# Seven sub-convolutions at the points of a polynomial product, in place of nine even/odd ones

## The reference

```
xc = x.T
h  = relu(bn1(conv1d(xc, conv1_w, kernel 1)))
h  = bn2(conv1d(h, conv2_w, kernel 17, pad 8))
x_conv = relu(h + xc).T
A  = exp(-dist(x @ w_se.T + b_se)) * adj ;  x_nmp = A @ relu(x @ w_msg.T + b_msg)
y  = GRU gates of [x_conv, x_nmp] against x          # tanh and sigmoid, three gates
x  = layernorm(x + y)
x  = layernorm(x + relu(((1 + eps) x + adj @ x) @ W1 + b1) @ W2 + b2)
```

## Time and profile before

| | us |
|---|---|
| median of 3 runs (393.55 to 393.71) | 393.56 |
| the profiled execution | 394.27 |
| its span, first to last instruction | 392.5 |
| TensorE / VectorE / ScalarE / GpSimd busy | 377.3 / 280.3 / 232.9 / 230.3 |
| one full step | 46.3 |
| start of step 1, end of step 7 | 36.9, 359.7 |

### The profile page before, as it was taken

How to read it: one execution, slowest core, us unless ns; L and a number is a source line. 1 busy time by engine, 2 the same in 40 slices (tenths; PEclk the granted TensorE clock), 3 DMA queues, 4 the chain that set the end, 5 groups by cost and what they waited for, 6 DMA issues and landing times.

```text
span 392.5 us, 6585 instructions
## 1 busy us (share of the span) xinstructions
PE 377.3 (96%) x2329; PEld 336.0 (86%) x2329; DVE 280.3 (71%) x545; ACT 232.9 (59%) x422; POOL 230.3 (59%) x217
## 2 busy tenths in 40 slices
PE   2999999999999999999999999999999999999974
PEld 2988989898889989899898988899898998988954
DVE  4999958864787658867598657885588675857564
ACT  3663584557654675737655478446766476462773
POOL 4886446574484934946366655657349483475343
PEclk9999999999999999999999999999999999999999
DMA  7503001201102101301012010120112110000011
GB/s 239 210 2 108 3 0 56 107 2 53 53 12 100 41 15 53 109 0 54 0 53 107 0 53 5 48 107 12 44 53 61 48 56 0 3 0 2 0 55 53
DMA packets 7991, 19.39 MB, mean 49 GB/s; under 512 B 672, under 2 KB 5024, under 8 KB 6944
## 3 DMA queue, kind: packets, MB, share of 16 engines
q1 hardware_dynamic: 7536, 18.50, 13.3%
q10 hardware_dynamic: 432, 0.59, 0.5%
HBM read 14.89 MB, written 4.19 MB: 49 GB/s over the span
## 4 chain that ended last, share of the span: by engine, by line
PE 95%; DVE 2%; DMA 1%; ACT 1%; POOL 0%; issue 0%; SPq 0%; ACTq 0%; DVEq 0%
PE conv L1129 31%; PE back L1129 30%; PE front L1231 7%; PE back L1231 7%; PE back L1320 6%; PE conv L1183 5%; PE front L1203 3%; PE front L1223 2%; PE back L1282 2%; DMA xv<-in_x_dram 1%; PE conv L1203 1%; PE front L1213 1%; PE front L1320 1%; ACT tail L693 1%; DVE xn L945 1%; PE front L1129 0%
## 5 line engine op out<-in xcount | busy, mean ns | idle before, releaser
L1129 PE MATMUL conv<-sth,wh 128*128 128x256 f32 x280 | 85.4, 305 | 0.0
L1129 PE MATMUL conv<-stl,wh 128*128 128x256 f32 x280 | 79.9, 285 | 0.0
L1129 PE MATMUL conv<-sth,wl 128*128 128x256 f32 x280 | 79.8, 285 | 0.0
L501 POOL TENSOR_TENSOR rstd<-rstd,minus_half 128x4 f32<-128x4 f32 (+1 forms) x34 | 36.1, 1063 | 60.6 <-DVE rstd L927 60.6
L506 POOL TENSOR_TENSOR xw<-xw,xv 128x512 f32<-128x512 f32 (+1 forms) x17 | 20.9, 1230 | 59.0 <-ACT xw L677 59.0
L1129 PEld LDWEIGHTS conv<-sth,wh 128*128 128x128 f32 x280 | 52.9, 189 | 1.6
L1129 PEld LDWEIGHTS conv<-stl,wh 128*128 128x128 f32 x280 | 52.9, 189 | 0.6
L1129 PEld LDWEIGHTS conv<-sth,wl 128*128 128x128 f32 x280 | 52.9, 189 | 0.0
L519 POOL TENSOR_TENSOR amat<-amat,adjT 128x512 f32<-128x512 f32 x32 | 48.8, 1547 | 0.8
L1231 PE MATMUL front<-amat,msg 128*128 128x256 f32 x128 | 30.2, 379 | 0.0
L1231 PE MATMUL back<-adjT,xn 128*128 128x256 f32 x120 | 29.2, 385 | 0.8 <-DVE xn L945 0.8
(11 more groups left out here) (217 smaller groups left out, 1018.5 us busy)
## 6 DMA issues: line engine op xcount, KB each, us to landing
adjT<-in_adj_dram SPq DMA_DIRECT2D x8, 1024.0 KB, 4.8
out_dram<-tail SPq DMA_DIRECT2D x15, 256.0 KB, 2.2
xv<-in_x_dram SPq DMA_DIRECT2D x7, 512.0 KB, 3.3
gbuf<-in_gates_dram SPq DMA_DIRECT2D x1, 576.0 KB, 7.0
tail<-in_conv_dram ACTq DMA_DIRECT2D x2, 256.0 KB, 3.7
xv<-in_x_dram SPq DMA_DIRECT2D x2, 256.0 KB, 4.7
later_w<-in_later_dram SPq DMA_DIRECT2D x1, 452.0 KB, 6.3
tail<-in_conv_dram SPq DMA_DIRECT2D x1, 320.0 KB, 5.3
```

The source lines that it names most:

```text
L501: done(pool.tensor_tensor(rstd[:, k, h, q], rstd[:, k, h, q], minus_half[:, q], ALU.pow), RSTD[k])
L1129: ins = pe.matmul(bank, a, b, start=first and k == 0, stop=last and k == len(todo) - 1)
```

## The change

The nine sub-convolutions become seven, by evaluating four-coefficient polynomials (four token phases, and the 17 taps in four phases) at 0, 1, -1, 2, -2, 1/2 and infinity. `NTAP` becomes (5, 5, 5, 5, 5, 5, 4): 34 taps. The streams are linear combinations of the phases of h1: `token_diffs` (two subtractions of 544 elements) and the sums and differences of `streams1`/`streams2` on GpSimd; `half_stream`, `zero_stream`, `parts2`, `parts1`, `inf_stream` on VectorE; five pairs of `stream_high` (ScalarE) and `stream_low` (VectorE) split them. The results are recombined with scales (`sc`, bn2's scale times constants) in `u_sum`, `pair2_sum`, `pair2_add`, `pair1_sum`, `pair1_add` and `inf_add` on VectorE, from two banks that ScalarE copies out twice each with different scales (`minus2_out`, `minus1_out`). The taps of each point are combined in the prologue (`taps_step`, and four sums on GpSimd). `hh` and `hl` move into the memory of `nmph` and `nmpl`. The lists of all engines are rewritten around it. Reference, DMAs of a step, gates, norms and MLP stay.

```diff
-NTAP = (5, 5, 4, 5, 5, 4, 4, 4, 4)
+HALF, ZERO, PLUS2, MINUS2, PLUS1, MINUS1, INF = range(7)
+POINTS = (0.5, 0.0, 2.0, -2.0, 1.0, -1.0)
+NTAP = (5, 5, 5, 5, 5, 5, 4)
...
+CONV_AT = ((0, 0), (0, 1), (1, 0), (1, 1), (2, 0), (2, 1), (1, 0))
...
 # GpSimd
+            def token_diffs(g, k0=0):
+                wait(pool, H1_READY, g, 2)
+                wait(pool, RI_READY, g - 1, 1)
+                (av[0:2] = h1[.., 1] - h1[.., 0];  av[2:4] = one_on(h1[.., 0]) - h1[.., 1])
+            def pair_streams(g, k, a, b, ready):
+                wait(pool, LS_READY, g - 1, (4, 3)[k - 1])
+                wait(pool, CONV_FULL[(MINUS1, MINUS2)[k - 1]], g - 1, 1)
+                (sv[r] = b + a;  sv[r + 1] = b - a)
 def steady:
+                streams1(gm)
                 residual(gb, 1 - u, 0)
-                split_diff(gm, 2)
                 residual(gb, 1 - u, 1)
...
                     mask(gm, u, b)
+                if front:
+                    token_diffs(s + 1)
                 rsqrt(1, gb, 0)
+                if front:
+                    streams2(s + 1)
                 rsqrt(1, gb, 1)
-                    (split_diff 0, diff_a, split_diff 1, diff_b)
...
 # ScalarE
+            def minus2_out(g):
+                wait(act, CONV_FULL[MINUS2], g, 1)
+                wait(act, ADD2_READY, g - 1, 2)
+                for k in range(2):
+                    done(act.activation(pm2[:, :, k, :], conv_out(MINUS2), ACT.Copy,
+                                        scale=sc[:, SC_MINUS2 + k:SC_MINUS2 + k + 1]), PM2_READY)
 def steady:
-                mm_out(gm)
                 for k in range(3):
                     msg_out(gm, k)
-                odd_high(gm, 1)
                 gates(gb, 0)
-                diff_high(gm, 1)
+                stream_high(gm, 3)
                 factors_out(gm)
                 gates(gb, 1)
-                odd_high(gm, 2)
-                diff_high(gm, 2)
-                am_out(gm)
+                minus2_out(gm)
+                stream_high(gm, 4)
                 if front:
                     x_high(gf, 1 - u)
-                bm_out(gm)
+                minus1_out(gm)
                 exps(gm, 0)
                 exps(gm, 1)
-                xconv_high(gm, 0)
                 h_high(gb, 0)
                 h_high(gb, 1)
+                xconv_high(gm, 0)
                 exps(gm, 2)
                 exps(gm, 3)
                 hidden(gb, 0)
                 hidden(gb, 1)
                 if front:
                     h1_out(gf, 0)
+                    h1_out(gf, 1)
+                    stream_high(gf, 0)
+                    stream_high(gf, 1)
                 nmp_high(gm, 0)
...
 # VectorE
+            def u_sum(g, u):
+                wait(dve, CONV_FULL[HALF], g, 1)
+                wait(dve, CONV_FULL[ZERO], g, 1)
+                (four scalar_tensor_tensor: usum phase k = HALF * scale k + x phase k; one adds ZERO to phase 0)
+            def pair2_sum(g):
+                wait(dve, PM2_READY, g, 2)
+                (two scalar_tensor_tensor: pm2[k] += PLUS2 * scale k)
 def steady:
+                parts1(gm)
+                u_sum(gm, u)
                 for k in range(3):
                     messages(gm, k)
                 factors(gm)
-                odd_low(gm, 1)
                 gates(gb, 1 - u, 0)
-                diff_low(gm, 1)
+                stream_low(gm, 3)
                 gates_end(gb, 0)
-                m_sum(gm)
+                inf_stream(gm)
                 gates(gb, 1 - u, 1)
                 y_stats(gb, 0)
-                odd_low(gm, 2)
+                pair2_sum(gm)
                 gates_end(gb, 1)
                 y_apply(gb, 0)
+                pair2_add(gm)
                 y_stats(gb, 1)
-                diff_low(gm, 2)
-                x_sum(gm, u, 0)
+                stream_low(gm, 4)
                 y_apply(gb, 1)
-                x_sum(gm, u, 1)
-                g_sum(gm, 0)
-                pre_sum(gm, 0)
+                pair1_sum(gm)
                 h_low(gb, 0)
                 h_low(gb, 1)
-                xconv_low(gm, 0)
+                pair1_add(gm, 0)
                 (x_low(gf) 0 and 1)
+                pair1_add(gm, 1)
+                xconv_low(gm, 0)
                 out_stats(gb, 0)
                 out_stats(gb, 1)
+                (if front: half_stream, zero_stream, stream_low 0, parts2, stream_low 1, all of gf)
                 nmp_low(gm, 0)
+                inf_add(gm)
+                (if front: stream_low(gf, 2))
+                nmp_low(gm, 1)
+                xconv_low(gm, 1)
...
 # TensorE
 def steady:
-                (taps 0, 1, 2)
+                (taps HALF, ZERO, PLUS2)
                 (messages, gates(gb, 0), factors, gates(gb, 1), y_transpose(gb, 0))
-                taps(gm, 3)
-                taps(gm, 4)
+                taps(gm, MINUS2)
+                taps(gm, PLUS1)
                 y_transpose(gb, 1)
-                taps(gm, 5)
-                taps(gm, 6)
+                taps(gm, MINUS1)
                 (distances 0 and 1, aggregate(gb, 0))
-                taps(gm, 7, 0, 2)
+                taps(gm, INF, 0, 1)
                 (aggregate(gb, 1), distances 2 and 3)
-                taps(gm, 7, 2, 3)
+                taps(gm, INF, 1, 2)
                 mlp1(gb, 0)
                 mlp1(gb, 1)
+                (conv1(gf, 0), mlp2(gb, 0), conv1(gf, 1), mlp2(gb, 1), nmp(gm, 0))
+                taps(gm, INF, 2)
+                nmp(gm, 1)
```

More of the change, by code:

```diff
@@ new lines, in pair2_sum, with pair2_add @@
+            def pair2_sum(g):
+                wait(dve, PM2_READY, g, 2)
+                for k in range(2):
+                    done(dve.scalar_tensor_tensor(pm2[:, :, k, :], conv_out(PLUS2), sc[:, SC_PLUS2 + k:SC_PLUS2 + k + 1],
+                                                  pm2[:, :, k, :], ALU.mult, ALU.add), SD2_READY)
+            def pair2_add(g):
+                wait(dve, SD2_READY, g, 2)
+                wait(dve, U_READY, g, 5)
+                u01, u23 = (graph_rows(usum[:, :, :, :])[:, q, :, :] for q in range(2))
+                both = pm2[:, :, :, :].rearrange("p b r m -> p (b r) m")
+                done(dve.tensor_tensor(u01, u01, both, ALU.add), ADD2_READY)
+                done(dve.scalar_tensor_tensor(u23, both, 4.0, u23, ALU.mult, ALU.add), ADD2_READY)
@@ L897, in xconv_low, with inf_add @@
+            def inf_add(g):
+                wait(dve, CONV_FULL[INF], g, 1)
+                wait(dve, PRE_READY, g, 2)
+                done(dve.scalar_tensor_tensor(phase(usum[:, :, :, :], 3), conv_out(INF), sc[:, SC_INF:SC_INF + 1],
+                                              phase(usum[:, :, :, :], 3), ALU.mult, ALU.add), PRE_READY)
             def xconv_low(g, par):
@@ L1018, in prologue @@
                     messages(0, k)
+                taps_step(utaps[:, 0:4, :], w2, 4.0, w0)
+                taps_step(ataps[:, 5:9, :], w3, 4.0, w1)
+                taps_step(gtaps[:, 5:9, :], ataps[:, 5:9, :], 2.0, utaps[:, 0:4, :])
+                taps_step(ataps[:, 5:9, :], ataps[:, 5:9, :], -2.0, utaps[:, 0:4, :])
+                parts1(0)
                 factors(0)
-                tap_low(0)
+                tap_low(ZERO)
+                tap_low(HALF)
+                dve.wait_ge(tap_sums, steps[0])
+                u_sum(0, 0)
                 x_low(1, 1, 0)
                 x_low(1, 1, 1)
-                tap_low(1)
-                tap_low(2)
-                m_sum(0)
+                tap_low(PLUS2)
+                inf_stream(0)
+                pair2_sum(0)
+                pair2_add(0)
+                tap_low(PLUS1)
                 w_low_part(wl[:, S_GATE:S_GATE + 9, :], graw, wh[:, S_GATE:S_GATE + 9, :], w_count("gates"))
                 w_low_part(w1l[:, :], w1raw, w1h[:, :], w_count("w1"))
-                x_sum(0, 0, 0)
-                x_sum(0, 0, 1)
-                g_sum(0, 0)
-                pre_sum(0, 0)
-                tap_low(3)
-                tap_low(6)
-                odd_low(1, 0)
+                pair1_sum(0)
+                pair1_add(0, 0)
+                pair1_add(0, 1)
+                half_stream(1)
+                zero_stream(1)
                 xconv_low(0, 0)
-                diff_low(1, 0)
+                stream_low(1, 0)
+                parts2(1)
+                stream_low(1, 1)
                 nmp_low(0, 0)
+                inf_add(0)
                 dve.wait_ge(consts_loaded, 16)
```

558 lines of the change are left out of this document (279 added, 279 removed).

## The result

| | before | after |
|---|---|---|
| median, us | 393.63 (393.55 to 394.52, 4 runs) | 428.98 (428.78 to 429.13, 4 runs) |
| span of the profiled execution | 392.5 | 427.0 |
| start of step 1 | 36.9 | 46.7 |
| a full step | 46.30 | 49.54 |

The changed kernel takes 1.0892 times as long (95% interval 1.0873 to 1.0911): 35.4 us more, with the forecast at 420.0 and its own band at 412 to 426. TensorE does less and the kernel is slower. The page after, to be laid beside the earlier trace rows: first the busy times, then the last chain by engine.

A forecast was written before the change was run, and what follows sets the result against it. TensorE was taken to bound the kernel, 96% busy. Forecast: 393.56 + 15.4 (seven steps) + 8.1 (first group) + 2.4 (step 1) + 0.5 (end) = 420.0 us; forecast band 412 to 426, range 405 to 430.

The forecast's parts named there:

- saved on TensorE, a step: Matmuls of each step: 40 taps become 34, saving 2.2 us a step, 15.5 in seven steps.
- wait 1: Second y_transpose: TensorE waits 1.4 us a step because pair2_sum stands ahead of gates_end(gb, 1) on VectorE.
- wait 2: Second aggregate: TensorE waits 1.1 us a step for y_apply, behind the new pair2_add on VectorE.
- wait 3: Last product of mlp1: TensorE waits 1.7 us a step for ScalarE's hidden, behind xconv_high.
- wait 4: Last product of gates(gb, 0): TensorE waits 0.3 us a step for the first tanh, between 0 and 0.9.
- more in step 1: Step 1: late messages raise the gates wait from 0.3 to some 2.3, PLUS2 stream 0.4 late: +2.4 us.
- the step sum: Each step: waits of 4.5 us against 2.2 to 2.3 saved, +2.2 a step, +15.4 in seven.
- The first group: Before step 1: VectorE's fuller list, slowed beside GpSimd, starts step 1 at 45 (36.8 to 47.4), +8.1 us.
- VectorE's share: VectorE in a full step: work rises from 33 to 39 us, over 80% busy in the changed profile.
- Rival C: Steps: VectorE, slowed by turns with GpSimd, becomes the bound; step 49.5 to 50.5, 426 to 433 us; chance 0.12.
- Rival B: Waits in the steps, but the first group's sums run unslowed and hidden: 406 to 409 us; chance 0.12.
- rival A: Whole kernel: TensorE stays the bound and the waits don't arise, 375.6 us; chance 0.14.

The follow-up runs named there:

- all_orders: Changed kernel with pair2 sums later and messages before parts1 and u_sum on VectorE, and xconv_high behind hidden(gb, 0) on ScalarE: 405.54 us, ratio 1.0279.
- apply_early: all_orders with stream_low(gm, 4), pair2_sum and y_apply(gb, 1) ahead of pair2_add on VectorE: 391.92 us, ratio 0.9925.
- short_masks0: Changed kernel with GpSimd's mask product of group 0 alone cut to one column: 427.03 us, ratio 1.0841.
- the last order: sums_first with the roundings of the last fourteen taps moved from ahead of step 1's messages to later in VectorE's list: 387.36 us, ratio 0.9838.
- pair2_last: Changed kernel with pair2_sum and pair2_add moved behind gates_end(gb, 1), y_apply(gb, 0) and y_stats(gb, 1) on VectorE: 422.14 us, ratio 1.0706.
- sums_first: streams_first with pair1_sum, pair1_add and inf_add of group 0 ahead of the roundings on VectorE: 390.94 us, ratio 0.9916.
- streams_first: first_early with the third stream of group 1 also ahead of W1's rounding and the first group's last sums: 391.13 us, ratio 0.9927.
- first_early: apply_early with group 1's conv1, token differences and streams moved earlier in the lists ahead of step 1: 391.06 us, ratio 0.9922.

## Why the prediction was right, and where it was short

The sign and the mechanism were right: the four waits, each at its place, and each gone when the order is changed. The size was 35.4 instead of 26.4, which lies outside the forecast's own 412 to 426. Term by term, in the traces:

| step of the forecast | forecast | measured |
|---|---|---|
| saved on TensorE, a step | 2.2 | 2.0 |
| wait 1, y_transpose | 1.4 | 1.51 |
| wait 2, aggregate | 1.1 | 0.71 |
| wait 3, mlp1 | 1.7 | 1.47 |
| wait 4, gates | 0.3 | 0.85 |
| restart behind the four waits | none | 0.7 |
| a full step against before | +2.2 | +3.24 |
| seven steps | +15.4 | +22.7 |
| start of step 1 | +8.1 | +9.8 |
| more in step 1 | +2.4 | +1.8 |
| end | +0.5 | +0.2 |

The waits are the totals above by their number; the aggregate's is without the 0.8 behind the last step. The last four rows add up to 34.5, the difference of the two profiled executions; the medians differ by 35.4 because the profiled execution of the kernel before (394.27) was 0.6 above its median and that of the changed kernel 0.2 below.

**The sum of the waits** was right: 4.5 forecast, 4.54 measured. That it is right to 0.04 is luck: wait 4 was under-sized and wait 2 over-sized by about as much. At wait 2 the second aggregate started 5.99 us after the second transpose (230.57 and 224.58), where the forecast had 6.2, and TensorE was ready after 5.2 and not 5.0. For wait 4 the timeline of VectorE shows why (start, us):

```profile
252.11 2.21 DVE L858 SCALAR_TENSOR_TENSOR bv<-h 128x272 f32<-128x272 f32 x3
...
256.97 0.55 DVE L880 TENSOR_TENSOR msg<-front,later_w 128x384 f32<-128x384 f32 x1
```

The three sums of 272 in parts1 took 2.21 us with GpSimd's products running beside them until 253.67; with the messages ahead of them, in all_orders, no GpSimd instruction ran beside them and they took 1.14. I had 3.6 us for parts1 and u_sum; it was 4.9.

**What failed is the step sum**: "4.5 against 2.2 to 2.3 saved" took an idle time as the price of a wait. With 4.55 us idle, TensorE should have been busy for 44.30 of the step, as in apply_early; it shows 44.99. The last matmul ahead of a wait is counted to its end, some 0.16 us beyond the point where the next would have started; the first one behind it stands for longer (0.50 against 0.39 at the gates, 0.63 against 0.60 at the transpose), and the next starts later. This cost beside the idle time is the restart of the table: 0.7 a step, 4.8 in all, beside 0.2 a step that the taps saved less. Together they are most of the 7.3 us by which the steps were missed.

**The first group** was taken at 45 within 36.8 to 47.4, and came at 46.7, near the end at which nearly everything runs slowed. The forecast had "gate and w1 lows 1.8 to 3.3" and "four tap lows ... 3.2 to 5.4", so 2.6 to 4.7 for the first two and one of the four; these took 5.8 (4.29 + 1.55), beyond the slow end, and short_masks0 puts that down to GpSimd.

**In step 1** the +2.4 came out near the measured +1.8, but not as it was told. There is no wait at the gates of step 1. TensorE ran its first 27 matmuls there at half clock, 2.4 us longer (last section), and so came to the gates' last product just as the tanh was ready (ScalarE, then TensorE):

```profile
61.07 0.68 ACT L673 ACTIVATE gbuf<-back,gbias 128x512 f32<-128x512 f32 x1
...
61.80 0.50 PE L1213 MATMUL back<-nmph,wh 128*128 128x512 f32 x1
```

The part that the forecast had right is VectorE's late messages, which set this point; the slow matmuls filled the wait of some 2.3 us that it expected, and the two didn't add up.

**The sign of VectorE's share failed.** "Over 80% busy" came out at 74% (36.75 of 49.54), because the step was longer and VectorE's time in it grew by 3.8 us where 6 were expected. With the same instructions it was 38.5 of 44.3 in apply_early, near the 39 of the forecast.

By the Trainium skill's rule (SBUF — State Buffer, section Who interferes with whom) the forecast had given 427 for the whole, nearer than 420.0. The rule agrees with the rows of the first group (4.29 against 2.12) and with parts1 (2.21 against 1.14). But blocking is not how the 35 us came about: 23.4 of them went by three orders and 37.1 by those of apply_early, with the same work on both engines.

**Rival C** named the measured time (426 to 433, a step of 49.5 to 50.5), which the forecast's band did not, with a wrong cause for the steps. It wanted VectorE's work to be the limit; in apply_early that work is the same and the step is 44.3. Parts of it hold: parts1, slowed by GpSimd, made wait 4 larger, and in the first group VectorE's list has next to no gap and every order only moved the stop. **Rival B** and **rival A** fell with the first group's +9.8 and the four waits.

Open is what a first group without GpSimd's interference would bring with the last order; that wasn't run.

## What to carry to other kernels

When a change takes work from the bound engine and puts it on others, walk each in-order list for an instruction that waits while a ready one, which the bound engine needs, stands behind it: here four such places turned a gain of 0.8% into a loss of 8.9%, and moving a handful of calls gave it back (1.6% with the first group's order). Look for the next wait behind the one that is taken out: pair2_last removed one and made another. Charge a wait at its idle time plus the restart, about 0.2 us each here. And tell the two kinds of bound apart by moving things: in the steps every reordering gained some 7 us or more, in the start-up none gained clearly until work left the list.

## What the runs showed of the hardware

TensorE fell to half clock behind gaps. Windows of the changed kernel behind its idle 3.12 us at 15.9 and behind the 5.25 us ahead of step 1:

```profile
16.00:20.50 4.50, 4.50 (x11) 3.60 (x12) 4.43 (x11) 2.39 (x5) 3.76 (x4) 0.50 0.00 0
```

```profile
46.72:52.62 5.90, 5.90 (x27) 5.90 (x28) 5.33 (x10) 3.43 (x6) 4.99 (x6) 0.50 0.00 0
```

The granted clock is 0.50 (1.2 GHz) in both. In the second, 27 matmuls start 0.213 us apart, at 0.123 later on: 2.4 us. In the forecast I had put 2 us at most on this. It did not decide the time: in sums_first the granted clock is 1.00 from 30 to 60 us, where it is 0.89 in streams_first, and the time fell by 0.2 us only, since VectorE set the pace. The short idle times of 0.7 to 1.5 us in the steps left the clock at 1.00.

GpSimd and VectorE slow each other: with GpSimd's masks and differences beside them (the changed kernel against short_masks0), two roundings of 640 and 1152 elements took 4.29 us instead of 2.12, a 512 sum 1.78 instead of 0.68, a 256 low 1.55 instead of 0.42. On GpSimd's side the two token differences of 544 elements took 1.33 and 1.92 us in first_early and 1.92 and 2.44 in all_orders, where the slowed roundings run beside them.
